# A graph, mixing and expert block on one core: the mixing weights' product made first, the value product ahead of the context, and 21 visits moved into the first layer

## What is computed

```python
xn = _layernorm(x)
def gnn_layer(x, W, b, src, dst):
    h = x @ W.T + b
    return relu(segment_sum(h[src], dst, num_segments=1250))
def mix(x):                                   # with Wq, Wk, Wv, W1, W2 of 512 x 512
    q = softmax(x @ Wq.T, axis=-1) * 512 ** -0.5
    k = softmax(x @ Wk.T, axis=-2)            # over the nodes
    context = k.T @ (x @ Wv.T)
    x = q @ context + x
    return x @ W1.T @ W2.T + x
x = x + gnn_layer(gnn_layer(xn, gW1, gb1), gW2, gb2) + mix(xn)
x = x + experts(_layernorm(x))                # Sinkhorn gates, top 156 nodes of each of 8 experts
```

## Time and profile before

| | |
|---|---|
| runs | 468.45, 468.71, 469.42 us; median 468.71 |
| profiled execution | 468.71 us, its span 467.0 us |
| mean granted TensorE clock | 0.996 |
| TensorE busy | 451.0 us (97%), 2418 products |
| VectorE busy | 320.9 us (69%) |
| ScalarE, GpSimd busy | 150.7 us (32%), 63.1 us (14%) |

### The profile page before, as it was taken

One profiled execution on the slowest core, in us unless ns is written; L12 is line 12 of the kernel. 1 busy time (PEld: TensorE's weight loads), 2 busy tenths in 40 slices (PEclk: granted clock), 3 DMA queues, 4 the chain that ended last, 5 costly groups with the idle time before them and its releaser, 6 DMA issues.

```text
span 467.0 us, 6804 instructions
## 1 busy us (share of the span) xinstructions
PE 451.0 (97%) x2418; PEld 360.8 (77%) x2418; DVE 320.9 (69%) x1104; ACT 150.7 (32%) x272; POOL 63.1 (14%) x90
## 2 busy tenths in 40 slices
PE   7999999999999999999999999999999999888995
PEld 4788778888888888888779999877777766654783
DVE  6995698898998988897752110444645666777972
ACT  4676453322323233342222110322133115551110
POOL 4088200000000000000004000002200000006642
PEclk9999999999999999999999999999999999989999
DMA  8902002921000000001200000002744449306891
GB/s 216 289 1 91 1 0 91 218 59 56 1 1 1 1 1 1 1 2 34 94 0 4 1 1 1 1 0 69 270 139 133 134 138 385 121 1 192 285 357 72
DMA packets 20846, 40.46 MB, mean 87 GB/s; under 512 B 2953, under 2 KB 3283, under 8 KB 20805
## 3 DMA queue, kind: packets, MB, share of 16 engines
q1 hardware_dynamic: 18549, 32.55, 22.4%
q0 software_dynamic: 2256, 7.39, 4.5%
HBM read 30.10 MB, written 10.31 MB: 87 GB/s over the span
## 4 chain that ended last, share of the span: by engine, by line
PE 86%; DVE 8%; ACT 2%; issue 1%; DMA 1%; SPq 0%; POOLq 0%; DVEq 0%
PE ps L736 46%; PE ps L1031 9%; PE ps L957 9%; PE ps L848 5%; PE ps L723 5%; PE ps L1048 2%; PE ps L1167 2%; ACT scrap_a L1424 1%; PE ps L1137 1%; PE ps L880 1%; DMA X<-in_x 1%; PE ps L770 1%; PE ps L984 1%; PE ps L1008 1%; PE ps L1078 1%
## 5 line engine op out<-in xcount | busy, mean ns | idle before, releaser
L1713 DVE TENSOR_SCALAR RING_D<-places,PLACES 125x170 bf16<-125x170 f16 (+1 forms) x239 | 61.9, 259 | 0.0
L1714 DVE TENSOR_SCALAR RING_S<-iota,HOME 125x128 bf16<-125x128 f16 x239 | 58.8, 246 | 0.0
L957 PE MATMUL ps<-AT,H1H 125*128 125x416 f32 (+1 forms) x108 | 38.0, 352 | 0.0
L957 PE MATMUL ps<-AT,H1L 125*128 125x416 f32 (+1 forms) x108 | 38.0, 351 | 0.0
L1031 PE MATMUL ps<-H2H,AT 125*125 125x512 f32 x90 | 36.1, 402 | 0.0
L1048 PE MATMUL ps<-WE0H 128*128 128x512 f32 x123 | 35.6, 423 | 0.0
L1031 PE MATMUL ps<-H2L,AT 125*125 125x512 f32 x90 | 35.5, 394 | 0.0
L1781 DVE TENSOR_TENSOR ps<-ps,bias 125x512 f32<-125x512 f32 x20 | 14.0, 699 | 28.0 <-PE ps L736 28.0
L1860 DVE SCALAR_TENSOR_TENSOR ZL<-ps,ZH 128x416 fp32r<-128x416 f32 (+1 forms) x12 | 6.3, 584 | 38.7 <-ACT ZH L1369 38.7
L723 PEld LDWEIGHTS ps<-RING_D,RING_S 125*125 125x125 bf16 x239 | 25.7, 136 | 7.9
L605 POOL TENSOR_TENSOR G2L<-RAW_G,G2H 128x512 fp32r<-128x512 f32 x4 | 5.0, 1286 | 192.2 <-ACT G2H L1186 192.2
(11 more groups left out here) (410 smaller groups left out, 1171.7 us busy)
## 6 DMA issues: line engine op xcount, KB each, us to landing
RAW_E<-in_experts SPq DMA_DIRECT2D x8, 1024.0 KB, 9.7
RAW_AGAIN<-in_experts SPq DMA_DIRECT2D x3, 1024.0 KB
X<-in_x SPq DMA_DIRECT2D x1, 2240.0 KB
out_x<-X SPq DMA_DIRECT2D x10, 224.0 KB
scratch<-X SPq DMA_DIRECT2D x10, 224.0 KB
scratch<-Y SPq DMA_DIRECT2D x10, 224.0 KB
RAW_K<-in_WkT SPq DMA_DIRECT2D x4, 256.0 KB, 4.3
RAW<-in_mW2T SPq DMA_DIRECT2D x1, 1024.0 KB, 12.2
```

What stands on the lines that cost most here:

```text
L957: pe.matmul(place(f), h[0:TT, k, 128 * f:128 * (f + 1)], AT[0:TT, k, c0:c1], start=(k == 0 and n == 0), stop=False)
L1713: V.tensor_scalar(hot_d(v, width(b)), places[0:ET, 0:width(b)], PLACES[0:ET, c:c + 1], None, ALU.is_equal)
L1714: V.tensor_scalar(hot_s(v), iota[0:ET, :], HOME[0:ET, c:c + 1], None, ALU.is_equal).then_inc(done["marked"], 1)
```

## The change

- W1 and W2 are loaded by chunks of 128 rows ahead of x, and TensorE makes the mixing product first, chunk by chunk into four banks at once; the fourth chunk and the identity follow the first transposes of x. Its rounding and remainders are among the first key tiles' work on ScalarE and VectorE. The remainders of W2 are the first on GpSimd, those of W1 on VectorE.
- The value product takes the place that the mixing product had, between the key tiles and the context totals. Wv is split during the key tiles.
- The last two tiles of the context totals go bank by bank, and the contexts go chunk by chunk over four banks, with the chunks of visits at every sixth pass.
- WQ's remainders are made on GpSimd instead of VectorE.
- The visits: 24 ahead of the queries instead of 45; 44 in the first layer instead of 23, two ahead of each tile and three at its middle, and `mark_next(2)` there.
- The gate sums are no longer made at the start, but from a column of ones in the second layer's gate products. Nine warm-up products instead of 12 and 4.

```diff
+MIX_BANKS, VALUE_BANKS = (6, 2, 7, 3), (6, 7, 0, 1)
 RING_A, RING_B = 6, 16
 AGAIN = 2
 WHOLE = 1.5 * 2.0 ** 23
-WARM, WARMER = 12, 8
+WARM = 9
...
+    for c, b in enumerate(MIX_BANKS):
+        use(f"mp{c}", (b,), ("mph_ready", c + 1), ("mpl_ready", c + 1))
...
-        use(f"mp{c}", (4, 5, 6), ("mph_ready", c + 1), ("mpl_ready", c + 1))
+        use(f"vp{c}", (4, 5, 6), ("vph_ready", c + 1), ("vpl_ready", c + 1))
...
+    use("ks", (5,), ("krs_ready", 1))
+    for c, b in enumerate(VALUE_BANKS):
+        use(f"cp{c}", (b,), ("cph_ready", c + 1), ("cpl_ready", c + 1))
...
-    spots = [("vp0", 6, 3)]
-    for u in ("vp1", "vp2", "vp3", "cp0", "cp1", "cp2", "cp3"):
-        spots += [(u, n, 3) for n in (0, 6)]
+    spots = [("cp", n, 3) for n in range(0, 48, 6)]
     for i in range(NT + 1):
         if i < NT:
             spots += [(f"q{i}", 0, 4), (f"q{i}", 6, 4 if i % 4 == 1 else 3)]
         if i:
             spots += [(f"x{i - 1}", n, 3 if n == 12 else 4) for n in (0, 6, 12, 18)]
-    spots += [(f"h{i}", 6, 3) for i in range(NT)]
+    for i in range(NT - 1):
+        spots += [(f"h{i}", 0, 2), (f"h{i}", 6, 3)]
...
-        chunks = [(n, c) for n in splits for c in range(C)]
-        by_dve = [("wk", 0), ("wk", 3), ("w1", 1), ("w1", 3)] + [(n, c) for n in ("wv", "wq", "g1") for c in range(C)]
+        chunks = [(n, c) for c in range(C) for n in ("w1", "w2")] + [(n, c) for n in ("wk", "wv", "wq", "g1", "g2") for c in range(C)]
+        by_dve = [("w1", c) for c in range(C)] + [("wk", 0), ("wk", 3), ("wv", 1), ("wv", 3)] + [("g1", c) for c in range(C)]
...
+            def load_pair(c):
+                f = slice(128 * c, 128 * (c + 1))
+                sp.dma_start(RAW_A[:, c, :], mW1[f, :]).then_inc(ld_pair[c] if c else loads["first_w1"], 16)
+                sp.dma_start(RAW_2[:, c, :], mW2T[f, :]).then_inc(ld_pair[c], 16)
...
+            for c in range(C - 1):
+                load_pair(c)
             load_x(0)
+            load_pair(C - 1)
             load_wk(0)
             load_wk(1)
             load_x(1)
-            sp.dma_start(gw1[:], rows(gate_w[0])).then_inc(loads["gate1"], 16)
             load_wk(2)
             load_wk(3)
             for part in range(2, len(PARTS)):
...
-            load_weight("w2", mW2T)
-            load_weight("w1", mW1)
...
+                split_lo("w2", c)
...
-            split_lo("w1", 0)
-            split_lo("w1", 2)
+            split_lo("wv", 0)
+            split_lo("wv", 2)
             for i in range(4, NT):
                 rest_of_x(i)
-            reads(pool, f"mp{C - 1}")
+            reads(pool, f"k{NT - 1}")
+            pool.wait_ge(done["xnl_ready"], NT)
...
+            def mix_weights(c, f, a, b, first=False, last=False):
+                w = ((W1H, W1L)[a], (W2H, W2L)[b])
+                return pe.matmul(PS[plan[f"mp{f}"][0]][:], w[0][:, c, 128 * f:128 * (f + 1)], w[1][:, c, :], start=first, stop=last)
+
+            for c in range(C - 1):
+                pe.wait_ge(*hi_of("w2", c))
+                for f in range(C):
+                    mix_weights(c, f, 0, 0, first=(c == 0))
+                pe.wait_ge(*lo_of("w1", c))
+                for f in range(C):
+                    mix_weights(c, f, 1, 0)
+                pe.wait_ge(*lo_of("w2", c))
+                for f in range(C):
+                    mix_weights(c, f, 0, 1)
+            pe.wait_ge(done["consts"], 1)
             turn_x(0)
-            pe.wait_ge(loads["gate1"], 16)
-            ps = opens("gsums")
-            for c in range(C):
-                mm = pe.matmul(ps[0:TT, 0:NE], ones[:, 0:TT], gw1[:, c, :], start=(c == 0), stop=(c == C - 1))
-            closes("gsums", mm)
-            warm(WARMER - 4)
+            pe.wait_ge(*lo_of("w1", C - 1))
+            pe.wait_ge(*lo_of("w2", C - 1))
+            for f in range(C):
+                mix_weights(C - 1, f, 0, 0)
+                pe.matmul(PS[plan[f"mp{f}"][0]][:, 128 * f:128 * (f + 1)], ident[:], ident[:], start=False, stop=False)
+                mix_weights(C - 1, f, 1, 0)
+                closes(f"mp{f}", mix_weights(C - 1, f, 0, 1, last=True))
+
             for i in range(NT):
                 pe.wait_ge(done["xtl_ready"], i + 1)
-                inside = {0: (1, 4), 1: (2, 4), 2: (3, 5), 4: (5, 3)}.get(i)
+                inside = {0: (1, 4), 1: (2, 6), 2: (3, 5), 4: (5, 3)}.get(i)
...
+            pe.wait_ge(done["mpl_ready"], C)
             for c in range(C):
-                ps = opens(f"mp{c}")
-
-                def add_one(k):
-
-                    if k == 1:
-                        pe.matmul(ps[:, 128 * c:128 * (c + 1)], ident[:], ident[:], start=False, stop=False)
-
-                product(f"mp{c}", ps[:], (block_of(W1H, c), block_of(W1L, c)), (rows_of(W2H), rows_of(W2L)), before=add_one,
+                product(f"vp{c}", opens(f"vp{c}")[:], (block_of(WVH, c), block_of(WVL, c)), (rows_of(MPH), rows_of(MPL)),
...
+            for i in range(NT - 2):
                 for c in range(C):
-                    ps = opens(f"tt{c}") if i == 0 else PS[plan[f"tt{c}"][0]]
-                    f = slice(128 * c, 128 * (c + 1))
-                    for n, (x, e) in enumerate(((XNH, EH), (XNH, EL), (XNL, EH))):
-                        mm = pe.matmul(ps[:], x[0:TT, i, f], e[0:TT, i % 4, :], start=(i == 0 and n == 0),
-                                       stop=(i == NT - 1 and n == 2))
-                    if i == NT - 1:
-                        closes(f"tt{c}", mm)
-                    elif c == C - 1:
-                        mm.then_inc(done["e_used"], 1)
-
-            for i in range(NT):
-                context(i)
+                    context(i, c)
                 if i == 1:
                     tile_ranks()
                 if i == 6:
                     chosen_tiles()
-                if i == NT - 2:
-                    pe.wait_ge(done["tiles_step"], 4)
-                    closes("flag", pe.matmul(opens("flag")[0:1, 0:1], over[0:TP, 0:1], ones[0:TP, 0:1], start=True, stop=True))
-
-            pe.wait_ge(*lo_of("wv", C - 1))
+            pe.wait_ge(done["tiles_step"], 4)
+            closes("flag", pe.matmul(opens("flag")[0:1, 0:1], over[0:TP, 0:1], ones[0:TP, 0:1], start=True, stop=True))
             for c in range(C):
-                product(f"vp{c}", opens(f"vp{c}")[:], (block_of(WVH, c), block_of(WVL, c)), (rows_of(MPH), rows_of(MPL)),
-                        unit=f"vp{c}")
-                if c == 0:
-                    pe.wait_ge(done["esum_step"], NT)
-                    ps = opens("ks")
-                    for f in range(C):
-                        mm = pe.matmul(ps[:, f:f + 1], ESUM[0:TT, 128 * f:128 * (f + 1)], ones[0:TT, 0:1], start=True, stop=True)
-                    closes("ks", mm)
+                for i in (NT - 2, NT - 1):
+                    context(i, c)
+
+            pe.wait_ge(done["esum_step"], NT)
+            ps = opens("ks")
+            for f in range(C):
+                mm = pe.matmul(ps[:, f:f + 1], ESUM[0:TT, 128 * f:128 * (f + 1)], ones[0:TT, 0:1], start=True, stop=True)
+            closes("ks", mm)
...
+            pe.wait_ge(done["vpl_ready"], C)
+            n = 0
             for c in range(C):
-                product(f"cp{c}", opens(f"cp{c}")[:], (block_of(TH, c), block_of(TL, c)), (rows_of(VPH), rows_of(VPL)),
-                        before=vp_ready if c == 0 else None, unit=f"cp{c}")
+                pe.wait_ge(done["tl_ready"], c + 1)
+                for f in range(C):
+                    ps = opens(f"cp{f}") if c == 0 else PS[plan[f"cp{f}"][0]]
+                    for k, (t, v) in enumerate(((TH, VPH), (TH, VPL), (TL, VPH))):
+                        visits("cp", n)
+                        n += 1
+                        mm = pe.matmul(ps[:], t[:, c, 128 * f:128 * (f + 1)], v[:, c, :], start=(c == 0 and k == 0),
+                                       stop=(c == C - 1 and k == 2))
+                    if c == C - 1:
+                        closes(f"cp{f}", mm)
...
+            def store_mix(c):
+                reads(act, f"mp{c}")
+                copy(MPH[:, c, :], ps_of(f"mp{c}")[:]).then_inc(done["mph_ready"], 1)
+
+            for c in range(C - 1):
+                split_hi("w1", c)
+                split_hi("w2", c)
             root(0)
+            split_hi("w1", C - 1)
+            split_hi("w2", C - 1)
             split_hi("wk", 0)
             split_hi("wk", 1)
             turned_x(0)
             root(1)
             split_hi("wk", 2)
             split_hi("wk", 3)
+            store_mix(0)
             turned_x(1)
+            store_mix(1)
             root(2)
+            store_mix(2)
             store_k(0)
+            store_mix(3)
...
-                groups_ending(f"vp{c}")
-                reads(act, f"vp{c}")
-                copy(VPH[:, c, :], ps_of(f"vp{c}")[:]).then_inc(done["vph_ready"], 1)
                 split_hi("wq", c)
+            groups_ending("cp", 0, 48)
...
+                split_lo("w1", c)
```

(54 more changed lines are left out.)

93 lines of the change are left out of this document (41 added, 52 removed).

## The result

| | before | after |
|---|---|---|
| median of 6 runs each | 469.12 us (468.45 to 471.35) | 499.77 us (498.87 to 500.14) |
| span of the profiled execution | 467.0 us | 498.4 us |
| mean granted TensorE clock | 0.996 | 0.979 |
| TensorE busy | 451.0 us (97%) | 463.0 us (93%) |

The ratio is 1.065, with an interval of 1.062 to 1.067: slower by 6.5%. The forecast was 494.3 in a range of 483 to 500.

A forecast was written before the change was run, and what follows sets the result against it. The prediction took TensorE, busy 97% of the span, as the bound. Its terms, -3.7 + 1.5 + 2.3 + 16.4 + 9.0 + 0.1 = +25.6 us, added to 468.7 gave 494.3 us, range 483 to 500.

The forecast's parts named there:

- Part 1: Mixing product moved to the front: second key tile starts at 21.2 instead of 13.18, net -3.7 us.
- Part 2: VectorE in the first key tiles: added subtractions and roundings make remainders late, +1.5 us, between 0 and 3.
- Part 3: Value product ahead of the contexts, and WQ's remainders moved to GpSimd: no net cost, 0.
- Part 4: All four contexts close together, so marks of the first query tile come late: +2.3 us, between 0.5 and 4.
- Part 5: 21 visits moved to the first layer: a loop between engines stalls TensorE each tile, +16.4 us, bounds 14 to 18.
- Part 6: Clock in the first-layer loop: six falls to the lower clock at 1.5 us, +9.0 us, between 0 and 12.
- Every pass starting at the low clock: In the first-layer loop, eight falls of the clock instead of six, the sum 3 us higher.
- Part 7: Gate sums by a ones column in the second layer: one small product and a tiny copy, +0.1 us.
- (a): Rival: the first-layer loop is there, but the clock holds; 485.3 us, chance 0.25.
- (b): Rival: not slower, the first layer's marks are never late because VectorE runs ahead; 467.0 us, chance 0.10.
- (c): Rival: at the front, weight chunks hold back x and key weights; +4 on the forecast, 498 us, chance 0.10.

The follow-up runs named there:

- move_only: Kernel before with only the visits and their marks moved, 21 visits more in the first layer; 495.58 us, ratio 1.059.
- marks_first: Changed kernel with the two marking calls ahead of the previous tile's remainder in the first layer; 487.54 us, ratio 1.041.
- lead4: Changed kernel with the marks of two more chunks made ahead of the first layer, four instead of two; 474.66 us, ratio 1.014.
- filled: Changed kernel with unused products behind first-layer tiles, five behind tile 0 and eight behind later ones; 492.46 us, ratio 1.050.
- best_qk: lead4 with WQ's remainders on VectorE, first query tile's marks ahead of context remainders, and two VectorE key-tile subtractions swapped; 468.09 us, ratio 0.9988.

## Why the prediction came out as it did

The direction, the cause of the greater part of the loss and the range were right; the time is 5.5 us over the forecast. That it lies in the range is close to luck: the median is 0.2 us under the upper end of 500, two of the six runs are above it, and a sixth fall of the clock, as in move_only, would have carried it out. The terms, in the prediction's order:

- **Part 1**, -3.7, came to -3.1: the second key tile starts at 21.82 instead of 21.2. The first four mixing products, 5.55 to 7.21, are the miss: they take 1.66 us where the prediction's 0.2325 each make 0.93. Their distance is near that of the lower clock (0.43), though the granted clock reads 1.00 from 5.5 to 7.0; what slowed them stays open.
- **Part 2**, +1.5, came to +1.6. The third key tile waits 0.59 for its operand (the prediction had 0.9) and the next transposes 0.41:

```profile
25.96 0.49 PE L743 MATMUL ps<-WKH,XTH 128*125 128x512 f32 x1 [0.59 <-DVE XTL L1536]
...
27.80 0.65 PE L776 MATMUL ps<-ident,XF 125*128 125x125 f32 x4 [0.41 <-DVE XF L1531]
```

- **Part 3**, 0, came to about +5.2 wait by wait (4.9 as the difference of the stages). This is the step that failed. Its sentence "GpSimd is idle there" looked at whether GpSimd had the time, and at when WQ's remainders are read. It did not ask what the subtractions do to VectorE, which at that hour makes marks that TensorE reads at once. 2.7 us of wait and 1.6 for a fall are theirs, and the runs with and without the load show them (4.3 us in their stage). The remaining 0.9 are longer waits for diag and EL, which were not tried by themselves. The trace of before held the warning, in rows that the prediction did not set side by side (the first of them stands in the earlier trace rows):

```profile
5.88 0.55 DVE L1497 TENSOR_SCALAR XF<-X,mv,rstd 125x512 f32<-125x512 f32 x1
...
9.50 1.28 DVE L1497 TENSOR_SCALAR XF<-X,mv,rstd 125x512 f32<-125x512 f32 x1
...
9.21 1.29 POOL L605 TENSOR_TENSOR WKL<-RAW_K,WKH 128x512 fp32r<-128x512 f32 x1 [0.78 <-ACT WKH L1186]
```

  The same operation on the same shape takes 0.55 alone and 1.28 when it starts while GpSimd subtracts. A group of instructions whose single times differ twofold is worth a look at what ran beside the slow ones. The Trainium skill (SBUF — State Buffer, "Who interferes with whom") has the rule: VectorE's tensor-scalar operations between SBUF operands in a two-port mode, and its operations with two SBUF inputs, share a port with GpSimd, and the one that comes second stands still for the other's whole instruction. The runs agree, with 0.77 beside 0.74 and 1.30 beside 1.3.
- **Part 4**, +2.3, came to +2.6: 1.2 ahead of the first query product and some 1.4 between there and the first layer.
- **Part 5**, +16.4, came to +16.6: the next tile's product comes 2.51 to 2.59 us behind the last issue, 2.53 in four of seven rounds, and the seven stalls make 15.0, with 1.61 for tile 1. The loop was walked out of rows of before and each member shows in the trace (the 0.05 for the signal has no row of its own); that it stalls once a tile rests on the fixed order of VectorE, and marks_first and lead4 confirm that.
- **Part 6**, +9.0 for six falls, came to +7.8 for five in the first layer. The size of one, 1.5, was nearly right. That there would be about this many was no more than a count taken from a range of 0 to 12: move_only had six from the same waits. The comparison behind it was of two measures: 60% is counted by the distances of the products, and the 2.77 of 4 us (69%) by busy time, in which a round without a fall has 3.60 of 5.48 us, 66%. Every pass starting at the low clock, which the prediction gave beside its sum as the rule of the Trainium skill (TensorE: Matmul & The Clock Gate, "HAM oscillation — how this bites in real kernels"), did not come: three of the eight rounds had no fall. The Trainium skill tells it there of waits for loads of about 3 to 5 us, longer than the 1.8 here, so it did not strictly speak of this loop.
- **Part 7**, +0.1: nothing to be seen.

The account: -3.1 + 1.6 + 5.2 + 2.6 + 16.6 + 7.8 is 30.7, and the 0.4 of the gap ahead of the adjacency products makes 31.1 of the 31.4. Against the forecast's +25.6, part 3 is the error, and part 6 took back 1.2 of it. Of the rivals, (a), the clock that holds, is what marks_first and filled make on purpose; it was not the case here. (b) would have needed two more chunks of lead, which lead4 shows: there the change costs 1.4% only, and WQ's place is most of that. (c) did not come.

A gain that the prediction did count, 3.7 us in front, shows in no version's time: best_qk is at most 0.3% under the kernel before. Small waits for VectorE stand against it (diag and EL 0.9 together more than before, XTL and XF, the first query tile), and the two edits made against them won 0.5 and 0.6 us where 1.0 was expected. How much each of them would give back if all were gone stays open.

## What to carry to other kernels

Work that costs TensorE the same wherever it stands can cost a round trip per tile once it is moved, if its operands are made by an engine whose fixed order puts them behind the close of the tile before: count the calls that produce against the chunks that consume, in tiles, not in chunks, and walk the loop once in the rows. When work goes to an idle engine, look for what it does to the busy ones that run beside it: compare the single times of the same operation with and without it. And where a loop leaves pauses, price the clock beside the wait; shortening the pause from 1.8 to 1.2 us gave back 12 us, of which only 4 were wait.

## What the runs showed of the hardware that was not expected

- A tensor-scalar operation of VectorE that normally takes 0.25 us takes 1.25 to 1.37 when it starts beside a GpSimd subtraction of 1.3 us, and 0.71 to 0.82 beside one of 0.74. A VectorE subtraction whose first input lies in PSUM is not held: in the kernel after it takes 0.68 at 15.75 us, with GpSimd's subtraction running from 15.12 to 16.40, whereas one with both inputs in SBUF takes 1.78 at 12.61, beside one that started at 12.49, instead of 0.69.

```profile
12.49 1.36 POOL L608 TENSOR_TENSOR W2L<-RAW,W2H 128x512 fp32r<-128x512 f32 x1 [1.11 <-ACT W2H L1209]
...
12.61 1.78 DVE L1543 TENSOR_TENSOR W1L<-RAW_A,W1H 128x512 fp32r<-128x512 f32 x1
...
15.12 1.28 POOL L608 TENSOR_TENSOR WKL<-RAW_K,WKH 128x512 fp32r<-128x512 f32 x1
...
15.75 0.68 DVE L1536 TENSOR_TENSOR XTL<-ps,XTH 128x500 fp32r<-128x500 f32 x1
```

- The loop with waits of 1.8 us (TensorE busy 3.60 of the 5.48 us of a round) had the clock fall in five of eight rounds; with waits of 1.2 us (3.61 of 4.82) it never fell in eight. At the third chunk of the contexts it fell behind two waits of 1.06 and 1.04 us in a row (98.74 to 101.50), so the length of a single wait does not decide it alone. What does was not separated.
- Five or eight more products that nobody reads, in each of these pauses, made the kernel 7.3 us faster.
